# Down weights kept as two rounded halves and rotated by two fp32r passes

## The reference, cut to what matters

```
x = L0_attn_x
x = _layernorm(x + _L0_attn_ref(x, ...), axis=-1)
# _L0_ffn_ref, x reshaped to 4096 x 512:
x = fwht(x * SU_ug) / SCALE
x_up   = x @ W_up.T   * (Wscale_ug[:INTER] * SCALE)
x_gate = x @ W_gate.T * (Wscale_ug[INTER:] * SCALE)
x = jax.nn.silu(x_gate) * x_up
x = fwht(x * SU_dp) / SCALE
x = x @ W_down.T * (Wscale_dp * SCALE)      # W_down: 512 x 2048
x = _layernorm(x + ..., axis=-1)
```

## Time and profile before

| what | us |
| --- | --- |
| median of 3 runs (1557.65 to 1559.36) | 1558.47 |
| the profiled execution | 1559.52 |
| its span | 1557.6 |
| PE busy in the span | 1523.6 |
| DVE, ACT, POOL busy | 1032.9, 625.5, 464.8 |
| attention ends, block 0 ends (about) | 519, 660 |

### The profile page before, as it was taken

The page is one execution under the profiler, slowest core; times in us unless marked ns, Lnnn a source line. Parts: engine busy times, 40 slices in busy tenths (PEclk is TensorE's granted clock), DMA queues, the critical chain, the costliest instruction groups (busy, mean ns, idle before and its releaser), DMA issues.

```text
span 1557.6 us, 26452 instructions
## 1 busy us (share of the span) xinstructions
PE 1523.6 (98%) x10152; PEld 1366.5 (88%) x10152; DVE 1032.9 (66%) x1790; ACT 625.5 (40%) x1289; POOL 464.8 (30%) x580
## 2 busy tenths in 40 slices
PE   6999999999999999999999999999999999999998
PEld 5977977888887888899999999999999999999997
DVE  6876786677687886864575575475566457557545
ACT  4163255236227655433333333333343333333322
POOL 5465456447338534500300030030030031003001
PEclk9999999999999999999999999999999999999999
DMA  7031122122122796677677668677766867766862
GB/s 282 1 114 70 35 82 101 35 82 102 64 68 101 282 378 256 243 261 290 225 249 283 235 214 292 224 247 251 269 228 232 295 213 256 274 235 219 288 220 94
DMA packets 92060, 307.44 MB, mean 197 GB/s; under 512 B 9888, under 2 KB 10272, under 8 KB 90144
## 3 DMA queue, kind: packets, MB, share of 16 engines
q1 hardware_dynamic: 90928, 301.54, 54.5%
q10 hardware_dynamic: 1008, 4.20, 0.7%
HBM read 255.37 MB, written 50.33 MB: 196 GB/s over the span
## 4 chain that ended last, share of the span: by engine, by line
PE 63%; DVE 4%; ACT 1%; issue 1%; POOL 1%; POOLq 0%; DVEq 0%; ACTq 0%
PE ff_bank_b L2056 17%; PE ff_bank_a L2056 11%; PE ff_bank_c L2056 11%; PE ff_acc L2083 7%; PE ff_acc L2084 7%; PE ff_acc L2076 7%; DVE ff_d_lo L1773 2%; PE ff_x_ps L2027 1%; PE ff_x_ps L2007 1%; ACT at_union L601 1%; PE ff_x_ps L2015 0%; PE ff_x_ps L2016 0%; DVE ff_c L1824 0%; DVE ff_h_lo L1792 0%; DVE ff_c L1820 0%
## 5 line engine op out<-in xcount | busy, mean ns | idle before, releaser
L2056 PE MATMUL ff_bank_b<-ff_x_hi,ff_ring 128*128 128x256 f32 x1536 | 302.6, 280 | 2.3 <-DVE ff_c L1824 1.8
L2056 PEld LDWEIGHTS ff_bank_b<-ff_x_hi,ff_ring 128*128 128x128 f32 x1536 | 247.8, 188 | 3.7 <-issue 3.5
L2056 PE MATMUL ff_bank_b<-ff_x_lo,ff_ring 128*128 128x256 f32 x768 | 214.3, 279 | 0.0
L2056 PE MATMUL ff_bank_c<-ff_x_hi,ff_ring 128*128 128x256 f32 x1024 | 204.0, 282 | 0.0
L2056 PE MATMUL ff_bank_a<-ff_x_hi,ff_ring 128*128 128x256 f32 x1024 | 203.5, 282 | 0.0
L2083 PE MATMUL ff_acc<-ff_d_lo,ff_h_hi 128*128 128x512 f32 x504 | 198.3, 393 | 2.2 <-DVE ff_d_lo L1773 2.2
L2084 PE MATMUL ff_acc<-ff_d_hi,ff_h_lo 128*128 128x512 f32 x504 | 196.2, 389 | 0.0
L2056 PEld LDWEIGHTS ff_bank_a<-ff_x_hi,ff_ring 128*128 128x128 f32 x1024 | 165.3, 188 | 2.7 <-issue 0.2
L2056 PEld LDWEIGHTS ff_bank_c<-ff_x_hi,ff_ring 128*128 128x128 f32 x1024 | 165.2, 188 | 2.1 <-issue 2.1
L1820 DVE TENSOR_TENSOR ff_c<-ff_bank_b,ff_c 128x512 f32<-128x512 f32 x64 | 44.2, 691 | 175.6 <-PE ff_bank_b L2056 174.4
L2056 PEld LDWEIGHTS ff_bank_b<-ff_x_lo,ff_ring 128*128 128x128 f32 x768 | 143.8, 187 | 0.0
(11 more groups left out here) (323 smaller groups left out, 3467.2 us busy)
## 6 DMA issues: line engine op xcount, KB each, us to landing
ff_ring<-gu_scratch SPq DMA_DIRECT2D x392, 512.0 KB, 5.0
gu_scratch<-ff_ring SPq DMA_DIRECT2D x56, 512.0 KB, 4.3
at_xt<-in_xt SPq DMA_DIRECT2D x4, 2048.0 KB, 8.0
at_xn<-in_x SPq DMA_DIRECT2D x32, 256.0 KB, 2.9
x_scratch<-at_x SPq DMA_DIRECT2D x32, 256.0 KB, 2.0
ff_raw<-in_wgu SPq DMA_DIRECT2D x8, 1024.0 KB, 7.5
at_wd_a<-in_wd SPq DMA_DIRECT2D x8, 512.0 KB, 4.1
mixed_scratch<-at_wd_a SPq DMA_DIRECT2D x8, 512.0 KB, 3.2
```

What stands on the lines that cost most here:

```text
L2056: i = pe.matmul(bank[:, m, :], r[:, a, m, c, :], b[:, k, c, :], start=(k < 3 and m == 0 and c == 0 and b is x_hi and a == 0), stop=(m == 1 ...
```

## The change

**Down weights in halves.** After POOL's four stages (and, for k = 0, a multiplication that POOL now does itself, `scale_down(b)`), ACT rounds the piece to fp32r into `wd_b` (`round_down`), POOL takes the low half into `wd_a` (`lower_down`), and SP stores both: 1 MB per piece, and wd_mixed counts to 22 instead of 18. SP's store of piece 0 now stands ahead of the token stores, the load of piece 1 after tile 0, not 1; in the last batch the second store stands after the first five product stores.

**Loaded by pairs.** `wd` becomes two buffers `down_in` of two chunks each, both halves. Pairs 0 and 1 are loaded at the start of feed-forward, pair p+1 at the end of step p, behind the raw weights of p+2; a pair is two DMAs of 512 KB in runs of 512 bytes (two chunks x 64 columns) where the load before had runs of 2 KB. Mixed chunks go to new tiles `wd_first` and `wd_second`.

**Rotated by two passes.** PE's fp32 matmul per chunk becomes two fp32r matmuls, Hadamard x hi and Hadamard x lo.

**Pooled low half.** In round i = 5 of every sequence `pooled_lo` stands between the two maxima.

```diff
                 def store_down(k):
-                    sp.wait_ge(*wd_mixed.now(b, 9 * k + 9))
-                    sp.dma_start(mixed_dram[b * 2 + k], wd_a[:, :, :]).then_inc(wd_out.sem, 16)
+                    sp.wait_ge(*wd_mixed.now(b, 11 * k + 10))
+                    sp.dma_start(mixed_dram[b * 2 + k, 0], wd_b[:, :, :]).then_inc(wd_out.sem, 16)
+                    sp.wait_ge(*wd_mixed.now(b, 11 * k + 11))
+                    sp.dma_start(mixed_dram[b * 2 + k, 1], wd_a[:, :, :]).then_inc(wd_out.sem, 16)
...
-            last_store = tiles(B - 1, False)
+            last_store, last_down = tiles(B - 1, False)
             ahead.store_first()
-            sp.wait_ge(*wd_out.now(B - 1, 32))
+            last_down()
+            sp.wait_ge(*wd_out.now(B - 1, 64))
...
+            def lower_down(b, k):
+
+                pool.wait_ge(*wd_mixed.now(b, 11 * k + 10))
+                pool.tensor_tensor(wd_a[:, :, :].bitcast(F32R), wd_a[:, :, :], wd_b[:, :, :], ALU.subtract).then_inc(wd_mixed.sem, 1)
...
+                scale_down(b)
                 split_x(b, 3)
+                lower_down(b, 0)
...
                 if more:
                     split_x(b + 1, 0)
                     split_x(b + 1, 1)
-                else:
+                lower_down(b, 1)
+                if not more:
                     return lambda: inverse_deviation(b, TILES - 1)
...
+            def round_down(b, k):
+                act.wait_ge(*wd_mixed.now(b, 11 * k + 9))
+                act.activation(wd_b[:, :, :].bitcast(F32R), wd_a[:, :, :], ACT.Copy).then_inc(wd_mixed.sem, 1)
...
+                        elif i == 5:
+                            local_maxima(i, (0,))
+                            pooled_lo(b, RT)
+                            local_maxima(i, (1,))
                         elif i:
                             local_maxima(i)
-                        if i == 5:
-                            pooled_lo(b, RT)
...
-            def down_weights(n):
-                half = slice(IC // 2 * n, IC // 2 * n + IC // 2)
-                sp.dma_start(wd[:, :, half, :], mixed_dram[:, :, half, :].rearrange("w p i n -> p w i n")).then_inc(wd_in[n], 16)
+            def down_weights(pair):
+                if pair >= 2:
+                    sp.wait_ge(w_had, 2 * pair - 2)
+                for h in range(2):
+                    sp.dma_start(down_in[pair % 2][:, h].bitcast(F32),
+                                 mixed_dram[:, h, :, 2 * pair:2 * pair + 2, :].rearrange("w p i n -> p w i n")).then_inc(wd_in[pair % 2], 16)
...
                             weights(p + 2)
+                        if k == MULS - 1 and 2 <= p + 1 < PAIRS:
+                            down_weights(p + 1)
...
-                pe.wait_ge(wd_in[i // 8], 16)
+                pe.wait_ge(wd_in[i // 2 % 2], 32 * (i // 4 + 1))
...
-                pe.matmul(x_ps[:, :], had[:, :], down_chunk(i), start=True, stop=True).then_inc(w_had, 1)
+                chunk = down_in[i // 2 % 2]
+                pe.matmul(x_ps[:, :], hr[:, :], chunk[:, 0, :, i % 2, :], start=True, stop=False)
+                pe.matmul(x_ps[:, :], hr[:, :], chunk[:, 1, :, i % 2, :], start=False, stop=True).then_inc(w_had, 1)
```

More of the change, by code:

```diff
@@ L328, in load_down @@
                         sp.wait_ge(wo_lo_s, 1)
-                    sp.wait_ge(*(wd_out.now(b, 16) if k else wd_out.last(b, 32)))
+                    sp.wait_ge(*(wd_out.now(b, 32) if k else wd_out.last(b, 64)))
                     sp.dma_start(wd_a[:, :, :], io["wd"][b * 2 + k]).then_inc(wd_in.sem, 16)
                 def store_down(k):
-                    sp.wait_ge(*wd_mixed.now(b, 9 * k + 9))
-                    sp.dma_start(mixed_dram[b * 2 + k], wd_a[:, :, :]).then_inc(wd_out.sem, 16)
+                    sp.wait_ge(*wd_mixed.now(b, 11 * k + 10))
+                    sp.dma_start(mixed_dram[b * 2 + k, 0], wd_b[:, :, :]).then_inc(wd_out.sem, 16)
+                    sp.wait_ge(*wd_mixed.now(b, 11 * k + 11))
+                    sp.dma_start(mixed_dram[b * 2 + k, 1], wd_a[:, :, :]).then_inc(wd_out.sem, 16)
                 load_down(0)
@@ L360, in tiles @@
                     if t == 0:
-                        store_down(0)
-                    if t == 1:
                         load_down(1)
-                    if t == RT:
+                    if fetch and t == RT:
                         store_down(1)
@@ L455, in mix_down, with scale_down @@
                 else:
-                    pool.wait_ge(*wd_mixed.now(b, 10 * k + 2 * stage))
+                    pool.wait_ge(*wd_mixed.now(b, 12 * k + 2 * stage))
                 pool.tensor_tensor(pair(dst)[:, :, 0], pair(src)[:, :, 0], pair(src)[:, :, 1], ALU.add).then_inc(wd_mixed.sem, 1)
                 pool.tensor_tensor(pair(dst)[:, :, 1], pair(src)[:, :, 0], pair(src)[:, :, 1], ALU.subtract).then_inc(wd_mixed.sem, 1)
+            def scale_down(b):
+                pool.wait_ge(held_in[0], 16)
+                pool.wait_ge(*wd_mixed.now(b, 8))
+                for h in range(2):
+                    v = wd_a[:, IC // 2 * h:IC // 2 * h + IC // 2, :]
+                    i = pool.tensor_tensor(v, v, bc(held["dps"][:, 2 * WC * b:2 * WC * b + WC], 1, IC // 2), ALU.mult)
+                i.then_inc(wd_mixed.sem, 1)
+            def lower_down(b, k):
+                pool.wait_ge(*wd_mixed.now(b, 11 * k + 10))
+                pool.tensor_tensor(wd_a[:, :, :].bitcast(F32R), wd_a[:, :, :], wd_b[:, :, :], ALU.subtract).then_inc(wd_mixed.sem, 1)
             def batch(b, more):
@@ L825, in batch, with scale_down @@
                     dve.tensor_tensor(vwo_lo[:, a, :], (acc, tr)[a][0:HK, :], vwo_hi[:, a, :].bitcast(F32), ALU.subtract).then_inc(vwo_lo_s.sem, 1)
-                def scale_down(k, halves):
-                    n = 2 * b + k
-                    dve.wait_ge(*(wd_in.now(b, 32) if k else wd_mixed.now(b, 8)))
+                def scale_down():
+                    dve.wait_ge(*wd_in.now(b, 32))
                     dve.wait_ge(held_in[0], 16)
-                    for h in halves:
+                    dve.wait_ge(*wd_mixed.now(b, 11))
+                    for h in range(2):
                         v = wd_a[:, IC // 2 * h:IC // 2 * h + IC // 2, :]
-                        i = dve.tensor_tensor(v, v, bc(held["dps"][:, WC * n:WC * n + WC], 1, IC // 2), ALU.mult)
-                    if halves[-1]:
-                        i.then_inc(wd_mixed.sem, 1)
+                        i = dve.tensor_tensor(v, v, bc(held["dps"][:, WC * (2 * b + 1):WC * (2 * b + 2)], 1, IC // 2), ALU.mult)
+                    i.then_inc(wd_mixed.sem, 1)
                 def softmax_in(t):
@@ L1298, in ffn_block @@
         sb, ps, signal, sem = tools(nc, ctx, sems, "ff")
-        wd = sb("wd", [P, WP, IC, WC])
+        down_in = [sb(f"down_in{i}", [P, 2, WP, 2, WC], F32R) for i in range(2)]
+        wd_first = sb("wd_first", [P, WP, IC // 2, WC])
         hr, hr_minus = sb("hr", [P, P], F32R), sb("hr_minus", [P, P], F32R)
```

18 lines of the change are left out of this document (11 added, 7 removed).

## The result

The changed kernel takes 1563.99 us (median of 6 runs, 1563.01 to 1567.09) against 1558.76 us for the kernel before, run beside it. The ratio is 1.0038, with a 95% interval of 1.0028 to 1.0048: slower by 4.4 to 7.5 us. The forecast was 1560.9, slower by 2.4 with 1553.8 to 1566.0 around it. The measured difference of the medians is 5.2 us. The sign and the two main losses (the late start of block 0, and pair 2 with the clock behind it) came true; the size was too small by 2.8 us, and two losses that were counted at nothing turned up.

What follows compares the result with a forecast made beforehand. PE bounds the kernel, busy 1523.6 of 1557.6 us. Terms -2.0 + 0 + 2.0 - 3.1 + 3.5 + 2.0 = +2.4 on 1558.47 gave 1560.9 us, range 1553.8 to 1566.

Steps and rivals of the forecast that it cites:

- Pooled low half: Attention, round 5 of each sequence: PE waits less for the low half behind one maximum; -2.0 us, bounds 0 and 2.5.
- POOL and ACT in attention: New multiplications and subtractions on POOL in each sequence may hold DVE's softmax; priced 0, up to +5 us.
- third of the prediction's own signs of being wrong: Attention: the softmax behind POOL's new subtraction turns up in PE's waits, against a price of 0.
- End of attention: Before block 0: the subtraction delays POOL's sums, which then lie across two DVE instructions; +2.0 us, bounds 0 and 2.6.
- Pair 2: Block 0, chunk 4: pair 2 lands at 558.1, PE idle 5.8 us; +3.5 us, bounds -1.2 and +10.
- the clock: Block 0, behind the idle time at chunk 4: PE runs at 1.2 GHz; +2.0 us, bounds 0 and 3.5.
- Later passes: Block 0, chunks 6 to 11, 14 and 15: two fp32r passes save 0.39 us each; -3.1 us, bounds 1 and 3.9.
- A: Rival: pair 2 lands in time, nothing waits and the clock stays; 1554.2 us, chance 0.20.
- B: Rival: the queue stays behind at pair 3, so PE waits again at chunk 6; 1565.4 us, chance 0.14.
- C: Rival: PE waits for pair 2 without a clock drop, 2.0 us less; 1558.9 us, chance 0.14.
- D: Rival: the passes save nothing since DVE, held by POOL, sets block 0's pace; 1564.0 us, chance 0.11.
- E: Rival: PE's low-half wait is unchanged, with L1235 waiting for something else there; 1562.9 us, chance 0.05.

Runs made afterwards that it cites:

- e3: Kernel before with only the pooled low half moved between the two maxima; 1557.82 us, ratio 0.9983 to 1.0001.
- e7: Changed kernel with block 1's tokens fetched at the end of step 1 and down weights laid out for 4 KB runs; 1560.24 us.
- e5: Changed kernel with the token-tile wait and block 1's token fetch (ff_y) moved to the end of step 1, behind pair 2's request; 1559.07 us.
- e6: Changed kernel with down weights laid out in DRAM by pairs, loaded in runs of 4 KB instead of 512 bytes; 1563.78 us.
- e10: e7 with pairs 3 to 7 requested sooner, block 1's tokens behind pair 3, and POOL's three sums for step 1 spread; 1556.60 us.
- e1: Changed kernel with pair p+1 requested at the first store of step p instead of at its end; 1560.69 us, ratio 1.0005 to 1.0022.
- e12: e10 with pair 2 also requested at the fourth store of its step, ahead of three stores and step 3's raw weights; 1555.06 us, ratio 0.9979.
- e8: e7 with each mix of a chunk done twice, four passes instead of two, the second pair overwriting the first; 1562.30 us.
- e4: Changed kernel with pairs requested early as in e1 and the last low half moved behind block 0's first split; 1560.66 us.

## Why the prediction was right, point by point

The sign was right, and the two largest losses are the ones forecast, for the reasons given. The size was too small, by terms counted at nothing or sized too low, as follows.

**Pooled low half, -2.0 forecast.** About -1.6 by the traces of e3. The three first sequences gave the 0.6 each; the last gave nothing where 0.2 was counted.

**POOL and ACT in attention, 0: +0.6.** In the changed kernel's profile the hold of DVE is hidden, but only because the stretch at the lower clock at 418 to 421.5 us had made PE late just ahead of the place. Of the ten other profiles with the halves nine show a wait of PE there, in the last sequence, 0.5 to 0.7 us in eight of them and 0.2 in e7; e5, which has none, has a stretch like that of the changed kernel. The kernels without the halves don't wait there. In e6:

```profile
426.52 2.81 POOL L471 TENSOR_TENSOR at_wd_a<-at_wd_a,h_dps 128x512 f32<-128x512 f32 x2
...
429.97 2.05 DVE L883 TENSOR_TENSOR at_sm<-at_sm,at_stat 128x192 f32<-128x192 f32 x1
...
431.77 2.46 POOL L477 TENSOR_TENSOR at_wd_a<-at_wd_a,at_wd_b 128x1024 fp32r<-128x1024 f32 x1
...
432.84 1.43 DVE L895 TENSOR_SCALAR at_stat<-at_stat,at_small 128x16 f32<-128x16 f32 x1
...
435.09 0.43 PE L1040 MATMUL at_mid<-h_ident,at_pr 128*104 128x128 f32 x2 [0.70 <-DVE at_pr L901]
```

In e3 the two instructions of DVE's softmax take 0.36 and 0.23 us. Here POOL's new multiplications (L471) push its split, which ends at 431.8, onto the first one, the new subtraction (L477) lies across the second, and PE came before the softmax was done. This is the third of the prediction's own signs of being wrong: it priced only the subtraction and counted on PE's queued projections as cover, and in the last sequence they were not enough. The other three sequences show no such wait, so it stays far below the 5 us of the bound.

**End of attention, +2.0.** 2.07 by the table (-2.09 to -0.02), for the reason given, and e10 shows the cause by removing it. tensor_tensor on SBUF took 1.68 instead of 0.69 us beside POOL, while its instructions that read PSUM were not held. The Trainium skill ("VectorE: DVE Perf Modes", Why `tensor_tensor` can't do 2×_2P or 4×) keeps this instruction out of the modes that spend both SBUF read ports on one tensor; the rows show it held beside POOL all the same.

**Pair 2, +3.5: +3.0, and the clock, +2.0: +3.0.** Forecast: landing at 558.1, PE idle for 5.8; measured 558.6 and 5.31. That the landing fits so well is partly luck: the raw weights ahead of the pair landed at 554.5, 0.6 us sooner than counted, and the pair's 1 MB took 4.0 us behind them where 3.0 was taken (3.9 in e6, in long runs). The clock term was sized too low. The lower level lasted 6.8 us, 6.2 of them with PE at work, and cost 3.0: the difference to before goes from +5.20 at chunk 4's first pass to +7.81, and the 0.39 that this chunk should have given back is gone as well. (The expectations of e1 and e5 say 2.4; that counts only from the matmul behind the chunk, at +5.38.) From +0.76 in step 1 to +6.74 at the down product of step 2 the two terms are 6.0 together, with the gains of chunks 3 to 5 taken off (that of chunk 2 went in step 1), where 5.5 was forecast.

**Step 1, counted at nothing: +0.8.** This step was missing. Between 521.6 and 542.4 PE lost 0.8 us, at 541.48 in a wait of 0.73 for DVE's ff_c. DVE stood behind two product instructions that POOL's sums now lay across. Before, and then after:

```profile
538.12 1.30 POOL L1487 TENSOR_TENSOR ff_sums<-ff_raw 128x512 f32<-128x512 f32 x1 [2.49 <-issue]
537.57 0.68 DVE L1768 TENSOR_TENSOR ff_ring<-ff_raw,ff_ring 128x512 fp32r<-128x512 f32 x1
538.97 0.99 DVE L1768 TENSOR_TENSOR ff_ring<-ff_sums,ff_ring 128x512 fp32r<-128x512 f32 x1 [0.72 <-ACT ff_ring L1612]
...
535.59 1.52 POOL L1519 TENSOR_TENSOR ff_sums<-ff_raw 128x512 f32<-128x512 f32 x1
537.45 1.57 DVE L1800 TENSOR_TENSOR ff_ring<-ff_raw,ff_ring 128x512 fp32r<-128x512 f32 x1
538.95 1.78 DVE L1800 TENSOR_TENSOR ff_ring<-ff_sums,ff_ring 128x512 fp32r<-128x512 f32 x1
```

The sums begin 2.5 us sooner because their raw weights do: issued at the same 529.0 in both, they took 9.0 us to land behind the 4 MB load and 6.1 behind the 2 MB that now stand there. The prediction let the smaller load speed up the token tile, and forgot what else it would speed up. No run tests this alone, but e12 agrees: there the first sum began at 536.45, DVE's two instructions took 0.93 and 1.24, and PE waited 0.17.

**Later passes, -3.1: -2.6** (+6.74 to +4.17). The ten chunks from 6 on give some 0.4 each, but PE, which comes sooner, waits longer for DVE at chunk 13 (2.04 instead of 1.65 us) and loses about 1 us ahead of chunk 14. The stretch at the lower clock near 643 us is not the cause: e6 has none there, waits instead, and ends alike (+6.80 to +4.07).

```profile
650.97 0.47 PE L2063 MATMUL ff_x_ps<-ff_down_in,ff_hr 128*128 128x512 f32 x1 [0.92 <-issue]
```

**The sum.** -1.6 + 0.6 + 2.1 + 0.8 + 3.0 + 3.0 - 2.6 = +5.3, against 2.4 forecast, 5.2 between the medians and 4.4 to 7.5 by the interval. The 2.9 us that the forecast lacked are 1.4 for the two steps counted at nothing, 1.0 for the clock, 0.4 for the low half, 0.1 for the end of attention and 0.5 for the later passes, less 0.5 for pair 2. The terms come from single profiles, so each may be off by some tenths, and the close match is in part luck. The chance stretches are outside this sum. The median of the mean granted clock is 0.9945 over the six runs of the changed kernel, and 0.998 to 0.999 over the kernel before beside the experiments; the stretch behind pair 2 takes 0.002 of that. The rest would be about one chance stretch more in each run; why, and what it adds, the runs don't settle.

**The rivals.** A (pair 2 in time) did not happen. B did not happen in the changed kernel, since the wait for pair 2 gave pair 3 the time, but came in e5 and e7 with 2.0 and 2.2 us. C is out, since the clock fell. D is out as it stands, though e8 shows less than half of the passes' time on the path. E is out, L1260 waits 0.28 where L1235 waited 0.90.

## What to carry to other kernels

Where all transfers share one queue that lands in order, price a new load by the bytes and waits that stand ahead of it, not by its own size or its runs, and look for what stands there without need; here a fetch that was used some 40 us later. And ask what a smaller load ahead will let start sooner. Requesting the new load earliest of all brought back 3.3 of 6.5 us (e1), and in e4 the delay went to those behind; the best kernel has it between the stores, with the other repairs (e12). And when an off-path engine gets an instruction more, look at what its neighbours in SBUF do in the shifted window: the same sums cost 2 us beside SBUF instructions and nothing beside those that read PSUM.

## What the runs showed of the hardware that was not expected

Issuing a transfer can itself hold SP. Pair 3, two transfers of 512 KB in runs of 512 bytes, took 7.26 us to issue in the changed kernel, 8.37 in e1 and 10.24 in e5; in runs of 4 KB it took 1.63 in e6 at the same place in the queue. A 256 KB tile behind a pair in short runs took 4.01 in e4, where it takes 0.32 in the changed kernel.

TensorE's clock drops to 1.2 GHz at few places, and not each time. All three profiles with a wait of more than 5 us for pair 2 have 6.8 us at the lower level behind it. The other stretches last 3.4 to 3.5 us, leaving out the last microseconds of a run. In block 0 there are five, each beginning within 1.3 us behind a wait of 1.8 to 2.5 us, and such waits stand in other profiles without a drop. In attention there are eight, and each begins as PE comes out of the same 32 matmuls of 48 columns, through which it was busy without a gap; this is from the changed kernel:

```profile
414.42 3.67 PE L1172 MATMUL at_mid<-at_ks_bd,at_wqs 128*128 128x48 f32 x32
417.91 0.61 PE L107 MATMUL at_acc<-at_wo_hi,at_tp_hi 128*104 128x512 f32 x1
```

These matmuls run once in each sequence, and in a profile the clock drops behind them in none, one or two of the four.
